# Cross attention of a two-layer kernel: 64-row halves for the key and value projections, units in both gaps of a round, and the loop over batches written out

## The reference

```python
q = (layernorm(x) @ Wq + bq)          # 64 x 256 for each batch
k = ctx @ Wk + bk                     # 1601 x 256, contraction over 192
v = ctx @ Wv + bv                     # 1601 x 256, contraction over 192
p = softmax(q_h @ k_h.T / sqrt(16))   # for each of 16 heads: 64 x 1601
x = x + concat_h(p @ v_h) @ Wo + bo
```

## Time and profile before

| | before |
|---|---|
| median of three runs | 3066.19 us (3065.31 to 3066.53) |
| the profiled execution | 3066.14 us, of which the span of the program is 3064.4 us |
| TensorE busy over the span | 2611.6 us (85%) |
| VectorE busy | 1781.3 us (58%) |
| ScalarE busy | 1084.1 us (35%) |
| GpSimd busy | 753.5 us (25%) |
| granted TensorE clock, mean | 0.918 |
| cross attention stage | about 30 to 970 us of the span |

### The profile page before, as it was taken

The page is one execution under the profiler, slowest core; times in us unless marked ns, Lnnn a source line. Parts: engine busy times, 40 slices in busy tenths (PEclk is TensorE's granted clock), DMA queues, the critical chain, the costliest instruction groups (busy, mean ns, idle before and its releaser), DMA issues. The chain is left out here.

```text
span 3064.4 us, 78538 instructions
## 1 busy us (share of the span) xinstructions
PE 2611.6 (85%) x34608; PEld 1894.5 (62%) x34608; DVE 1781.3 (58%) x2561; ACT 1084.1 (35%) x1702; POOL 753.5 (25%) x964
## 2 busy tenths in 40 slices
PE   5998988988897979988888878777688999888598
PEld 3565555555555545545555554443688898888487
DVE  4655545545454444569999975537666556665500
ACT  2443433434343211145555542216233333332121
POOL 6900000000000000012333323030565556663200
PEclk9999999989898779989999988889899998999699
DMA  2101001001000001132322201000000000000131
GB/s 63 33 18 34 18 18 34 18 18 32 20 2 22 0 26 36 50 94 66 93 71 82 82 17 48 0 20 14 3 4 3 4 4 4 4 3 3 55 137 41
DMA packets 24535, 99.16 MB, mean 32 GB/s; under 512 B 4824, under 2 KB 9837, under 8 KB 19502
## 3 DMA queue, kind: packets, MB, share of 16 engines
q1 hardware_dynamic: 24238, 94.57, 10.6%
HBM read 93.51 MB, written 1.05 MB: 31 GB/s over the span
## 5 line engine op out<-in xcount | busy, mean ns | idle before, releaser
L611 DVE TENSOR_REDUCE xa_minus_max_parts<-psum 128x4 f32<-128x1600 f32 (+1 forms) x128 | 233.9, 1827 | 221.9 <-PE psum L331 221.9
L628 DVE TENSOR_TENSOR xa_probT<-psum,xa_minus_max_spread 128x2048 f32<-128x2048 f32 (+1 forms) x112 | 239.6, 2139 | 200.5 <-PE psum L350 200.5
L315 PE MATMUL psum<-xa_ctxT,xa_wk 96*128 96x400 f32 (+1 forms) x512 | 217.7, 551 | 0.9 <-issue 0.8
L536 ACT ACTIVATE xa_probT<-xa_probT,zero_column 128x2048 f32<-128x2048 f32 (+1 forms) x112 | 209.4, 1870 | 10.8 <-DVE xa_probT L628 10.8
L2017 POOL TENSOR_TENSOR pa_cT<-pa_mt_and_qw,pa_levelT 128x256 f32<-128x256 f32 x256 | 192.6, 787 | 69.4 <-PE psum L2051 69.4
L322 PE MATMUL psum<-xa_wv,xa_ctxT 96*128 96x256 f32 (+1 forms) x832 | 208.0, 392 | 0.0
L1279 POOL TENSOR_TENSOR tk_exp_all<-tk_exp_all,tk_exp_left 128x577 f32<-128x577 f32 x64 | 120.9, 1890 | 354.2 <-ACT tk_exp_left L1400 354.2
L2189 ACT ACTIVATE pa_x<-psum 128x256 f32<-128x256 f32 x256 | 98.4, 384 | 306.3 <-PE psum L2051 294.1
L2265 DVE TENSOR_TENSOR pa_inv_and_invT<-pa_inv_and_invT,psum 128x512 f32<-128x512 f32 x192 | 132.0, 688 | 126.9 <-PE psum L2051 126.9
L716 POOL MEMSET la_v<- 128x512 f32 x1 | 0.5, 525 | 809.2 <-remote 809.2
L2051 PE MATMUL psum<-pa_inv_and_invT,pa_cT 64*64 64x64 f32 x4096 | 153.6, 237 | 40.3 <-DVE pa_prob L2226 36.7
(11 more groups left out here) (471 smaller groups left out, 5143.0 us busy)
## 6 DMA issues: line engine op xcount, KB each, us to landing
tk_ctx<-in_ctx SPq DMA_DIRECT2D x16, 1248.0 KB, 5.5
xa_ctxT<-in_ctxT SPq DMA_DIRECT2D x16, 1200.8 KB, 7.4
tk_ctxT<-in_ctxT SPq DMA_DIRECT2D x16, 1200.8 KB
ec_w<-in_ec_w SPq DMA_DIRECT2D x16, 1024.0 KB, 6.8
m_gate_up<-in_m_gate_up SPq DMA_DIRECT2D x17, 256.0 KB, 2.6
m_down<-in_m_down SPq DMA_DIRECT2D x17, 128.0 KB, 2.5
ff_w<-in_ff_w SPq DMA_DIRECT2D x2, 1024.0 KB
x_resident<-in_x SPq DMA_DIRECT2D x1, 1024.0 KB, 4.8
```

Of the source, the lines that this page charges most:

```text
L315: mm = mmul(ps[:, KEY_BANK[n], 0:z - a], wk[:, k, m * P:(m + 1) * P], ctxT[:, h, k, a:z], start=(k == 0), stop=(k == 1))
L536: a_(o, o, ACT.Exp, bias=core.zero[0:w]).then_inc(e_done, 1)
L611: v_.tensor_reduce(part[:, :, n % 2, n // 2], ps[:, 0:4, 0:z - a], AX.X, ALU.max, negate=True).then_inc(m_used, 1)
L628: v_.tensor_tensor(o[:, :, 0:chunks], got[:, :, 0:chunks], shift[0:w].unsqueeze(2).broadcast_to([w, 8, chunks, P]), ALU.add).then_inc(sub_ ...
```

## The change

Only `cross_attention` and the arrays made for it differ.

1. **64-row halves.** The contraction over 192 channels is now 3 thirds of 64 rows. Partitions 0 to 63 hold context rows 0 to 895, partitions 64 to 127 hold context rows 800 to 1600, each with the three thirds. `keys` and `values` issue for each third one matmul on rows 0 to 63 (bank 5) and one on rows 64 to 127 (bank 6), in turn. Both halves' results are copied out by one ScalarE instruction (128x2x400 for keys, 128x2x512 for values). There are 4 units of keys (3 x 2 matmuls of 400 columns) and 7 pairs of value chunks (3 x 2 matmuls of 256 columns), copied out in 4 + 4 instructions where there were 8 + 7.
2. **Units cut over both gaps.** In rounds 0 to 2 the first third of a unit of keys stands under `subtract`, the other two under `reduce`. In rounds 3 to 6 the first two thirds of a value pair stand under `subtract`, its last third and the next pair under `reduce`. The first unit of keys of a batch is made in `last_maximum` of the batch before.
3. **Maxima in two halves.** `spread_maximum` and `spread_out` go in two parts: for the first half of the heads in round 4, for the second at the end of the batch; 4 matmuls and one 128x512 copy each. `shift` has two slots. VectorE's small `maximum` goes twice.
4. **Placement.** All of `turn_out`, `turn_own`, `project` and the spread use bank 7. `turn_own` moves to the gap under `reduce` of round 3, `project` to that of round 5.
5. **Loop written out.** `batches` is a Python loop over all 16 batches; the loads on the SP queue are written out too.
6. **Data.** A context load has 128 x 2688 floats (1344 KB) in place of 96 x 3202 (1200.8 KB), `wk` and `wv` are twice as large (384 KB in place of 192 KB).

The path attention stage is the same text in both kernels.

```diff
-        wk, wv = sb("wk", [CH, 2, D]), sb("wv", [CH, 2, D])
+        wk, wv = sb("wk", [P, 3, D]), sb("wv", [P, 3, D])
-        ctxT = sb("ctxT", [CH, 2, 2, NK])
+        ctxT = sb("ctxT", [P, 2, 3, LOW * P])
...
-        def batches(eng, body):
-            body(0, 0, 0, True, False)
-            body(1, 0, 1, False, False)
-            with eng.Fori(1, TILES - 1) as i:
-                body(2 * i, i, 0, False, False)
-                body(2 * i + 1, i, 1, False, False)
-            body(B - 2, TILES - 1, 0, False, False)
-            body(B - 1, TILES - 1, 1, False, True)
+        def batches(body):
+            for n in range(B):
+                body(n, n // 2, n % 2, n == 0, n == B - 1)
...
-            def keys(h, n):
-                m, (a, z) = n % 2, PARTS[n // 2]
-                for k in range(2):
-                    mm = mmul(ps[:, KEY_BANK[n], 0:z - a], wk[:, k, m * P:(m + 1) * P], ctxT[:, h, k, a:z],
-                              start=(k == 0), stop=(k == 1))
-                mm.then_inc(k_ps, 1)
+            def keys(h, n, thirds):
+                m, (a, z) = n // 2, PARTS[n % 2]
+                for k in thirds:
+                    for half, rows in enumerate((slice(0, HALF), slice(HALF, P))):
+                        mm = mmul(ps[:, 5 + half, 0:z - a], wk[rows, k, m * P:(m + 1) * P], ctxT[rows, h, k, a:z],
+                                  start=(k == 0), stop=(k == 2))
+                if 2 in thirds:
+                    mm.then_inc(k_ps, 1)
+            def values(h, i, thirds):
+                for k in thirds:
+                    for half, rows in enumerate((slice(0, HALF), slice(HALF, P))):
+                        c = i + LOW * half
+                        if c >= KC:
+                            continue
+                        at = c * P - OVER * half
+                        mm = mmul(ps[0:width(c), 5 + half, i % 2 * D:(i % 2 + 1) * D], ctxT[rows, h, k, at:at + width(c)],
+                                  wv[rows, k, :], start=(k == 0), stop=(k == 2))
+                if 2 in thirds and i in (1, 3, 5, 6):
+                    mm.then_inc(v_ps, 1)
...
+            def under_shift(b, h, t):
+                if t < 3:
+                    pe.wait_ge(k_sb, 4 * b + t + 1)
+                    keys(h, t + 1, (0,))
+                else:
+                    pe.wait_ge(*((k_sb, 4 * b + 4) if t == 3 else (v_sb, 4 * b + t - 3)))
+                    values(h, 2 * (t - 3), (0, 1))
+            def under_maximum(b, h, t, tail, y):
+                if t < 3:
+                    keys(h, t + 1, (1, 2))
+                else:
+                    values(h, 2 * (t - 3), (2,))
+                    if t < 6:
+                        values(h, 2 * (t - 3) + 1, (0, 1, 2))
+                if t == 1 and tail:
+                    turn_out(b - 2)
+                if t == 3 and tail:
+                    turn_own(b - 2)
+                if t == 4:
                     if tail:
                         pe.wait_ge(oT_ready, 2 * (b - 1))
+                    spread_maximum(b, 0)
+                if t == 5 and y is not None:
+                    pe.wait_ge(n_sb, 2 * b + 1)
+                    project(y)
+            def last_maximum(b, h, y):
                 pe.wait_ge(m_used, MAXES * b + 7)
                 direct(b, h, 7)
+                if b + 1 < B:
+                    pe.wait_ge(ctx_loaded[1 - h], 16 * ((b + 1) // 2) + 16)
+                    pe.wait_ge(v_sb, 4 * b + 4)
+                    keys(1 - h, 0, (0, 1, 2))
+                pe.wait_ge(n_sb, 2 * b + 1)
+                if y is not None:
+                    pe.wait_ge(x_done, y + 1)
+                spread_maximum(b, 1)
```

More of the change, by code:

```diff
@@ L333, in direct, with spread_maximum @@
                 mm.then_inc(m_ps, 1)
[L335 to L339, removed]
+            def spread_maximum(b, r):
+                pe.wait_ge(max_step, 2 * b + r + 1)
+                for j in range(4):
+                    mm = mmul(ps[:, SIDE, j * P:(j + 1) * P], nmax[:, r, j:j + 1].broadcast_to([P, P]),
                               core.ident[:], start=True, stop=True)
@@ L381, in project @@
                 for e in range(2):
[L382 to L398, removed]
-                    if tail:
[L400 to L412, removed]
-                        pe.wait_ge(oT_ready, 2 * (b - 1))
[L414 to L417, removed]
@@ L445, in last_maximum @@
-            def last_maximum(b, h):
+                    mmul(ps[:, SIDE, 0:D], oT[:, e].rearrange("p h t -> p (h t)"), wo[:, e, :], start=(e == 0), stop=False)
+                mmul(ps[:, SIDE, 0:D], core.ones[:], bo[:], start=False, stop=True).then_inc(y_ps, 1)
+            def under_shift(b, h, t):
[5 more added lines that the diff above has]
+                    values(h, 2 * (t - 3), (0, 1))
@@ L470, in body @@
                         pe.wait_ge(sub_done, 7 * n + t)
-                        if not last:
-                            pe.wait_ge(m_used, MAXES * (n + 1) + t)
+                    if not last:
+                        pe.wait_ge(m_used, MAXES * (n + 1) + t)
+                    if t == 0 and last:
+                        pe.wait_ge(m_used, MAXES * (n + 1))
                     scores(n, h, t)
                     if t == 0:
-                        pe.wait_ge(v_sb, 7 * n + 7)
                         if not first:
@@ L492, in body @@
                         continue
-                    under_shift(n + 1, 1 - h, t, not first, None if first or h else i - 1)
+                    y = None if first or h else i - 1
+                    under_shift(n + 1, 1 - h, t)
                     pe.wait_ge(sub_done, 7 * n + t + 1)
                     direct(n + 1, 1 - h, t)
-                    under_maximum(n + 1, 1 - h, t, not first)
+                    under_maximum(n + 1, 1 - h, t, not first, y)
                 if not last:
-                    last_maximum(n + 1, 1 - h)
-            batches(pe, body)
+                    last_maximum(n + 1, 1 - h, y)
+            batches(body)
             pe.wait_ge(e_done, 7 * B)
@@ L576, in body @@
                         copy_out(n - 1)
-                    if t == 3 and not first:
-                        own_out(n - 1, 1 - h)
-                    if not last:
-                        under_shift(n + 1, 1 - h, t)
                     exponentials(n, h, t)
                     if not last:
-                        under_maximum(n + 1, 1 - h, t)
+                        between(n + 1, 1 - h, t)
+                    if t == 3 - last and not first:
+                        own_out(n - 1, 1 - h)
                 if not last:
                     last_maximum(n + 1, 1 - h)
-            batches(act, body)
+            batches(body)
             copy_out(B - 1)
@@ L646, in _ @@
                 reduce(0, n)
-            maximum(0)
+                if n == 3:
+                    maximum(0, 0)
+            maximum(0, 1)
             def body(n, i, h, first, last):
@@ L657, in body @@
                         reduce(n + 1, t)
+                        if t == 3:
+                            maximum(n + 1, 0)
                     if t == 1 and not first:
                         normalise(n - 1)
-                    if t == 4 and not first and not h:
+                    if t == 5 and not first and not h:
                         add(i - 1)
@@ L663, in body @@
                     reduce(n + 1, 7)
-                    maximum(n + 1)
-            batches(dve, body)
+                    maximum(n + 1, 1)
+            batches(body)
             normalise(B - 1)
```

151 lines of the change are left out of this document (64 added, 87 removed).

## The result

| | before | after |
|---|---|---|
| median | 3065.75 us (3060.88 to 3066.53, 4 runs) | 2977.69 us (2968.81 to 2980.99, 4 runs) |
| the profiled execution | 3066.14 us | 2980.99 us, span 2979.3 us |
| granted TensorE clock, mean | 0.918 | 0.923 |

The ratio is 0.9711, 95% interval 0.9698 to 0.9724: 88 us less, where 74 were forecast. The time lies 0.3 us under the forecast's range.

What follows compares the result with a forecast made beforehand. Cross attention was taken as bound by VectorE and TensorE in turn, plus loop turns. Loop -55.7, batches -21 and prologue +4 gave -73 us from 3066.1: 2993, stated as 2992, 80% range 2978 to 3026.

Steps and rivals of the forecast that it cites:

- the forecast's range: The 80% range for the changed kernel's time, 2978 to 3026 us.
- What bounds the kernel: Cross attention: a closed chain of VectorE and TensorE in turn, 6.66 us a round, plus about 55.7 us outside rounds.
- the loop's -55.7: Cross attention's batch loop written out: its five turns, with the slow clock behind them, go, -55.7 us in all.
- TensorE's price: Cost of projection matmuls: 0.68 us for 400 columns, 0.43 for 256, 0.18 for a change of matmul kind.
- the overlap of the halves: Two 64-row matmuls on alternating halves run at once, a pair at the price of one.
- The batch, -1.4 us, fifteen of them -21: Cross attention's rounds: each batch -1.3 us, -1.4 with `project` 0.1 cheaper in every other one; fifteen batches -21 us.
- the batch end: Round 6 to the next batch's subtract 0: 10.5 us in place of 12.21, -1.7 us a batch.
- that 0.14: In round 2, `direct` starts 0.14 us behind subtract's end; counted as part of the 6.66 us chain.
- Rival 1: Thin round 6 drops the clock at three to eight batch ends, about 5 us each: +15 to +40, 3007 to 3032; 20%.
- Prologue: Start of cross attention: each unit waits for the copy before it in banks 5 and 6; 40.4 us for 36.6, +4.
- Later stages, 0: The stages behind cross attention: no change in time, 0 us.
- the likeliest case: The forecast itself, 67%, with its own range of 2980 to 3003 us: rounds good to 0.5 us a batch, prologue to 4.

Runs made afterwards that it cites:

- e1: The kernel before with only the loop over batches written out; 3000.61 us, ratio 0.9802.
- e4: The changed kernel with the first half of the spread maxima (4 matmuls) moved from round 4 to round 6; 2949.49 us, ratio 0.9637.
- e9: The changed kernel with one memset of about 1 us added on VectorE at the start of path attention; 2980.47 us.
- e10: The changed kernel with two memsets, about 2 us, added on VectorE at the start of path attention; 2991.38 us.
- e6: The kernel before, loop kept, with each context load waiting for one more group of values, so it starts some 30 us into the next batch; 3015.28 us, ratio 0.985.

## Why the prediction was right and where it was wrong

- *What bounds the kernel, and the loop's -55.7*: right in size. e1 gives 56.2 in the batches. (The 7s that I read into cross attention's clock slices stand in slices 14 and 15, behind it; its own low ones are the 8s of 9, 11 and 13.) But the cause is not the loop alone: 40 of it are the place of the context load. "The five turns go" would have been the wrong advice had the load stood elsewhere.
- *TensorE's price and the overlap of the halves*: right. 12 records of 401 columns take 2.29 us in e4's trace, forecast 2.2; 16 records of 256 columns 2.00 us. The shortfall of row tiles that the Trainium skill's 3.07 for four suggests ("TensorE: Matmul & The Clock Gate", Part 3) is not seen: one, two and three pairs take 0.94, 1.62 and 2.29 us, so each further pair costs 0.67 to 0.68, the price of one matmul of 400 columns.
- *The batch, -1.4 us, fifteen of them -21*: this is the step that failed, by its size; the mechanism was right. Against e1's undisturbed 52.8 and 54.5 us the changed kernel has 50.3 and 51.6: -2.5 and -2.9, 40 us over fifteen. The parts, from one subtract to the next, measured with the forecast behind: round 0 -0.47 (-0.2), rounds 1 and 2 -0.09 each (0), round 3 -0.06 (+0.3), round 4 +0.45 (+0.7), round 5 -0.47 (-0.4), the batch end -1.78 (-1.7). `project` costs 7.44 - 6.06 = 1.38 us (1.6). Three mistakes: behind `direct` in rounds 3 and 4 I charged +0.36 and +1.05 us for `turn_own` and the spread, which cost 0.09 and 0.91 over the 6.57 us round; the written-out code has 7.05 in round 0, where I took 6.88 from the loop's; and the chain itself got shorter, 6.57 for 6.66, because the time from subtract to `direct` fell from 0.14 to 0.05 us. I had read that 0.14 as a hand-over. But in the earlier trace rows `direct` starts just as the 1.54 us of the unit ahead of it end and shows no wait for VectorE, while in the changed kernel TensorE idles 0.51 us there: 0.09 us of the old round were projection.
- *Rival 1, half clock at batch ends*, had a chance of 20% and came true: seven of fifteen ends, for the reason given. Its price of 5 us was too high by three times. I took it from batches that followed a 6 us wait; a drop behind a 1.3 us hole costs 1.6 us. 763.6 us undisturbed and 11.1 for the drops make the 774.7.
- *Prologue*: +5.0, forecast +4. It holds a clock drop at 78 us; e9, with the same stage and no drop there, has its first subtract at 82.6 us, +3.1. The waits for the single pair of banks are there: the timeline shows six of 1.02 to 1.12 us ahead of the units' first matmul.
- *Later stages, 0*: forecast as the same text and thus the same time. In the first trace they are 6.4 us shorter, nearly all in path attention. The change had no part in it that the runs show: the stage varies between 802.7 and 810.0 us over kernels that share its text, by 3.8 us between two traces of the kernel before, and e10 puts it 10 us the other way. So 6.4 us of the gain are luck, and without them the time would have come out near 2984 us.
- *The range*: its own bound for the likeliest case rested on "0.5 us a batch", and the error was 1.2 to 1.5, of which the drops took back 0.7. The likeliest case allowed 8 us for fifteen batches and nothing for later stages. The span fell by 12.4 us more than the terms' -72.7: 19 more in the batches, 11 given back by the drops, 6.4 in later stages, less 1.9 for the prologue and the last batch. Two misses cancelled in part.

```profile
45.02 0.94 PE L311 MATMUL psum<-xa_ctxT,xa_wk 64*128 64x400 f32 x4 [1.02 <-ACT xa_kT L506]
...
63.30 1.13 PE L324 MATMUL psum<-xa_wv,xa_ctxT 64*128 64x256 f32 x8 [1.12 <-ACT xa_v L515]
```

These two rows of the changed kernel's timeline are the first and the last but one of the prologue's waits for a copy.

## What to carry to other kernels

Where a hardware loop's turn shows a wait on nothing, look at what the DMA engines do at that moment, and at the instruction queue among them, before writing the loop out: moving one load took 48 us off the kernel before (ratio 0.985), for one number. Where two engines hand the same banks to and fro, put independent work where TensorE idles longest, not where there is room in the text: the same four matmuls cost 0.9 us in round 4, and in round 6 nothing, and they kept the clock up as well. And price a chain's hand-overs from a place where the waiting engine is idle: elsewhere its own work may hide in them.

## What the runs showed of the hardware that was not expected

- A loop's turn on TensorE waited 5.4 to 6.3 us with a 1200 KB load under way and 1.9 us at most without it (e6). A 16 KB packet of instructions came behind the load, and the first matmul 1.5 to 1.6 us behind the packet, in twenty turns of four traces.
- 64-row matmuls of a float32 unit overlap fully when issued two on one half and then two on the other (8 records of 400 columns in 1.62 us), and partly with three and three (2.53 for 2.00 us).
- One added matmul of 512 columns in a 1.3 us hole took 11 us off fifteen batches by keeping the clock at its higher level.
- A stage whose text never changed took 803 to 810 us, and with a 2 us pause put ahead of it 813 us (one trace).
